# Twelve instead of eight of the last 32 token tiles are summed on TensorE, twenty instead of 24 on VectorE

## The reference

```python
x = x + _L0_ffn_ref(_L0_cond_ref(x, cond_512, ...), ...)      # the last "x +" is the input itself

# inside _L0_ffn_ref:
topv, topi = jax.lax.top_k(glogits, TOPK)                     # TOPK = 4 of E = 32 experts
gw = jax.nn.softmax(topv, axis=-1)
combine = jnp.zeros((N, E), x.dtype).at[jnp.arange(N)[:, None], topi].add(gw)
def body(acc, we):
    wu, wd, ce = we
    ug = h2 @ wu
    u, g = (ug[:, :DFF], ug[:, DFF:])
    return (acc + ce[:, None] * (jax.nn.silu(g) * u @ wd), None)
y2, _ = jax.lax.scan(body, jnp.zeros_like(h2), (W_up, W_down, combine.T))
return x + y2.reshape(Bx, Tx, Dx)
```

## Time and profile before

| | |
|---|---|
| median of 3 runs | 1138.51 us (1137.43 to 1142.05) |
| the profiled execution | 1133.5 us, its span 1131.7 us |
| PE busy in the span | 984.0 us (87%) |
| DVE busy | 829.8 us (73%) |
| POOL busy | 700.9 us (62%) |
| ACT busy | 456.6 us (40%) |
| mean granted TensorE clock | 0.918 of full |
| DMA | 239.22 MB, mean 211 GB/s |

### The profile page before, as it was taken

The page is one execution under the profiler, slowest core; times in us unless marked ns, Lnnn a source line. Parts: engine busy times, 40 slices in busy tenths (PEclk is TensorE's granted clock), DMA queues, the critical chain, the costliest instruction groups (busy, mean ns, idle before and its releaser), DMA issues.

```text
span 1131.7 us, 19754 instructions
## 1 busy us (share of the span) xinstructions
PE 984.0 (87%) x6270; PEld 795.6 (70%) x6270; DVE 829.8 (73%) x1750; ACT 456.6 (40%) x1120; POOL 700.9 (62%) x654
## 2 busy tenths in 40 slices
PE   3879699998999989989987419999999999999995
PEld 2557477676776776757766308888888888888884
DVE  3878589778787788877957526777777677777778
ACT  1123243342432423333344205555555555555541
POOL 1404435757747667576585856777777777777750
PEclk8779799889898898988999659999999999999997
DMA  6237976566566555574665467776776767766599
GB/s 188 69 87 237 326 255 187 157 198 179 176 181 207 161 167 190 179 217 136 186 204 194 154 231 261 266 257 246 255 245 212 250 228 250 257 212 209 133 336 372
DMA packets 110748, 239.22 MB, mean 211 GB/s; under 512 B 19170, under 2 KB 48247, under 8 KB 109914
## 3 DMA queue, kind: packets, MB, share of 16 engines
q1 hardware_dynamic: 84042, 192.03, 51.8%
q0 software_dynamic: 19552, 40.02, 11.1%
q10 hardware_dynamic: 7056, 5.91, 1.6%
HBM read 140.37 MB, written 90.05 MB: 204 GB/s over the span
## 4 chain that ended last, share of the span: by engine, by line
PE 38%; DVE 22%; POOL 18%; issue 14%; DMA 6%; ACT 1%; SPq 0%; DVEq 0%; POOLq 0%; ACTq 0%
POOL rows_in L685 7%; PE gbank L985 7%; PE gbank L852 6%; DVE ring L1354 6%; POOL pick_rows L692 4%; POOL lists L647 4%; PE scores L813 4%; DMA rows_in<-x_rows,token_row 4%; PE gbank L1005 3%; PE gbank L777 3%; PE gbank L748 2%; POOL ring L654 1%; DVE stat L1368 1%; PE gbank L767 1%; DVE prob L1390 1%
## 5 line engine op out<-in xcount | busy, mean ns | idle before, releaser
L985 PE MATMUL gbank<-ring,in_part 128*128 x954 | 262.8, 411 | 0.1
L654 POOL TENSOR_TENSOR ring<-ring 128x512 fp32r<-128x512 f32 x96 | 121.5, 1281 | 141.7 <-ACT ring L1151 141.1
L692 POOL DMA_INDIRECT pick_rows<-rows_out,pair_row x156 | 161.6, 1036 | 56.5 <-issue 46.9
L985 PEld LDWEIGHTS gbank<-ring,in_part 128*128 128x128 f32 x954 | 168.6, 190 | 28.7 <-issue 0.3
L685 POOL DMA_INDIRECT rows_in<-x_rows,token_row x156 | 151.7, 972 | 54.2 <-issue 34.3
L647 POOL DMA_INDIRECT lists<-entry,slot_i x128 | 136.1, 1063 | 36.7 <-issue 34.1
L1005 PE MATMUL gbank<-ring,mid_part 128*128 x954 | 151.3, 294 | 0.4 <-DVE mid_part L1609 0.4
L1588 DVE SCALAR_TENSOR_TENSOR in_part<-scores,norm_w,in_part 128x128 fp32r<-128x128 f32 x318 | 96.8, 346 | 53.2 <-ACT in_part L1196 53.1
L1597 DVE SCALAR_TENSOR_TENSOR mid<-gbank,norms,silu 128x256 f32<-128x256 f32 x156 | 75.5, 484 | 74.4 <-ACT silu L1204 73.0
L852 PE MATMUL gbank<-w_o,ring 128*128 128x256 f32 x512 | 126.3, 403 | 0.6 <-ACT ring L1121 0.6
L777 PE MATMUL gbank<-h_t,w_qk 128*128 128x512 f32 x480 | 122.1, 405 | 4.7 <-DVE ring L1354 2.5
(11 more groups left out here) (171 smaller groups left out, 1553.1 us busy)
## 6 DMA issues: line engine op xcount, KB each, us to landing
w_parts<-ring SPq DMA_DIRECT2D x192, 256.0 KB, 3.2
ring<-w_parts SPq DMA_DIRECT2D x32, 1536.0 KB
ring<-in_W_up SPq DMA_DIRECT2D x64, 256.0 KB, 4.1
q_r<-rot SPq DMA_DIRECT2D x32, 512.0 KB, 6.1
picks<-pick_rows SPq DMA_DIRECT2D x8, 2048.0 KB, 22.2
lists<-in_fill_slots SPq DMA_DIRECT2D x36, 256.0 KB, 5.2
ring<-in_W_down SPq DMA_DIRECT2D x32, 256.0 KB, 3.9
x_t<-in_x_t SPq DMA_DIRECT2D x8, 512.0 KB, 4.9
```

Of the source, the lines that this page charges most:

```text
L654: e.tensor_tensor(lower, lower.bitcast(F32), upper.bitcast(F32), ALU.subtract).then_inc(s_lower, 1)
L692: e.indirect_dma_start(out=pick_rows, out_offset=bass.IndirectOffsetOnAxis(ap=begun_row[:, i:i + 1] if i < AHEAD else pair_row[:, i:i + 1] ...
L985: ins = e.matmul(bank[:, :], in_parts[i % 2][x][:, c, :], ring[:, bass.ds(at + y * WE + c * 2 * DFF, 2 * DFF)], start=k == 0, stop=k == le ...
```

## The change

A list says how many tiles of each part go to TensorE: 1, 2, 1, 2, 1, 2, 1, 2. These are the last tiles of the part (tile 3, or tiles 2 and 3), 12 in all. VectorE takes the first three or the first two. PE and ACT now loop over the 12 tiles, and SP's and VectorE's shapes follow. SP's condition for loading part 6 and 7 counts TensorE's tiles of the parts 0 and 0 to 1: 1 and 3, before 1 and 2.

```diff
+SUMS = [1 + c % 2 for c in range(PARTS)]
+SUMMED = [(c, c * NP + NP - n + k) for c, n in enumerate(SUMS) for k in range(n)]
@@ SP
             if c >= NPICK:
                 w.wait_ge(s_final, c - NPICK + 1)
-                w.wait_ge(s_sum, c - NPICK + 1)
+                w.wait_ge(s_sum, sum(SUMS[:c - NPICK + 1]))
...
-            e.dma_start(d["out"][c * NP * P:(c * NP + NP - 1) * P, :].rearrange("(t p) n -> p t n", p=P),
-                        resid[:, c * NP:c * NP + NP - 1, :]).then_inc(s_out, 16)
-        w.wait_ge(s_out, 16 * 2 * PARTS)
+            own = NP - SUMS[c]
+            e.dma_start(d["out"][c * NP * P:(c * NP + own) * P, :].rearrange("(t p) n -> p t n", p=P),
+                        resid[:, c * NP:c * NP + own, :]).then_inc(s_out, 16)
+        w.wait_ge(s_out, 16 * (PARTS + len(SUMMED)))
@@ PE
-        for c in range(PARTS):
-            bank, t = gbank[c % 2][:, 0:D], c * NP + NP - 1
-            if c >= 2:
-                w.wait_ge(s_summed, c - 1)
+        for n, (c, t) in enumerate(SUMMED):
+            bank = gbank[n % 2][:, 0:D]
+            if n >= 2:
+                w.wait_ge(s_summed, n - 1)
             w.wait_ge(s_resid, NT // NX)
             e.matmul(bank, ident[:, :], resid[:, t, :], start=True, stop=False)
             w.wait_ge(s_picks[c % NPICK], 16 * (c // NPICK + 1))
             for k in range(TOPK):
-                ins = e.matmul(bank, ident[:, :], picks[c % NPICK][:, NP - 1, k, :], start=False, stop=k == TOPK - 1)
+                ins = e.matmul(bank, ident[:, :], picks[c % NPICK][:, t % NP, k, :], start=False, stop=k == TOPK - 1)
             ins.then_inc(s_sum, 1)
@@ ACT
-        for c in range(PARTS):
-            t = c * NP + NP - 1
-            w.wait_ge(s_sum, c + 1)
-            e.activation(resid[:, t, :], gbank[c % 2][:, 0:D], ACT.Copy).then_inc(s_summed, 1)
-            w.wait_ge(s_summed, c + 1)
+        for n, (c, t) in enumerate(SUMMED):
+            w.wait_ge(s_sum, n + 1)
+            e.activation(resid[:, t, :], gbank[n % 2][:, 0:D], ACT.Copy).then_inc(s_summed, 1)
+            w.wait_ge(s_summed, n + 1)
             e.dma_start(d["out"][t * P:(t + 1) * P, :], resid[:, t, :]).then_inc(s_out, 16)
@@ DVE
-            at = slice(c * NP, c * NP + NP - 1)
+            n = NP - SUMS[c]
+            at = slice(c * NP, c * NP + n)
```

More of the change, by code:

```diff
@@ L1634, in vector_program @@
             w.wait_ge(s_picks[c % NPICK], 16 * (c // NPICK + 1))
-            at = slice(c * NP, c * NP + NP - 1)
-            half = own.mark(e.tensor_tensor(pk[:, 0:NP - 1, 0:2, :], pk[:, 0:NP - 1, 0:2, :], pk[:, 0:NP - 1, 2:4, :], ALU.add))
+            n = NP - SUMS[c]
+            at = slice(c * NP, c * NP + n)
+            half = own.mark(e.tensor_tensor(pk[:, 0:n, 0:2, :], pk[:, 0:n, 0:2, :], pk[:, 0:n, 2:4, :], ALU.add))
             w.wait_ge(s_vector, half)
-            whole = own.mark(e.tensor_tensor(pk[:, 0:NP - 1, 0, :], pk[:, 0:NP - 1, 0, :], pk[:, 0:NP - 1, 1, :], ALU.add))
+            whole = own.mark(e.tensor_tensor(pk[:, 0:n, 0, :], pk[:, 0:n, 0, :], pk[:, 0:n, 1, :], ALU.add))
             w.wait_ge(s_back, 16)
             w.wait_ge(s_vector, whole)
-            e.tensor_tensor(resid[:, at, :], resid[:, at, :], pk[:, 0:NP - 1, 0, :], ALU.add).then_inc(s_final, 1)
+            e.tensor_tensor(resid[:, at, :], resid[:, at, :], pk[:, 0:n, 0, :], ALU.add).then_inc(s_final, 1)
     banks_for = banks_of()
```

## The result

The changed kernel takes 1140.03 us (median of 14 runs, 1137.07 to 1148.15) against 1136.99 us for the kernel before (14 runs, 1134.31 to 1142.05): +3.0 us, a ratio of 1.0032 with a 95% interval of 1.0016 to 1.0047. The profiled execution took 1137.89 us, its span 1136.1 us. Forecast were 1142.9 us, +4.4 us, and 1136.1 us for the span.

What follows compares the result with a forecast made beforehand. VectorE and the DMA engines were taken as both at their limit; TensorE would then end last: +5.3 + 0.46 - 1.3 = +4.4 us, 1137.9 against the profiled 1133.5, carried to the median 1142.9 us, range 1138.5 to 1147.

Steps and rivals of the forecast that it cites:

- VectorE saves 4.2 us: VectorE's additions at the end: four parts shrink from three tiles to two, 1.05 us saved each, ending at 1123.5.
- None of the extra tiles fits into TensorE's idle 5.68 us, since ACT is not free: TensorE's third tile: both banks full at 1103.86, it still waits for ACT, and ACT for the scatters.
- Ten tiles behind the release, 4 x 2.16 us on the path less 3.3 of slack: TensorE after ACT's first copy: ten tiles instead of six, ending 8.6 us later at 1133.0, 5.3 past VectorE's old end.
- The last landing, 2.3 us: Final 128 KB output, issued at 1133.45: lands in 2.3 us, bounds 1.7 and 5.2.
- Part 7's load, late but free: SP's load, issued 7.8 us late at about 1113.5, lands at about 1121; cost nothing, bounds 0 to 1.5 us.
- The other signs: ACT's first copy near 1109, ten gapless tiles, final chain through TensorE, load issued at 1113.5 without holding TensorE, DMA full until 1128.
- TensorE wants part 7 at 1130.7: TensorE's eleventh tile needs that load at 1109.54 + 3.86 + 8 x 2.16; even a landing at 1129.8 wouldn't hold TensorE.
- rival (C): Part 7's late load sets the end if landing takes over 17 us; at 20 us, 3 us more, 1146; chance 0.05.
- Sum +4.4 us: Whole kernel: +5.3 for TensorE's tiles, +0.46 to the last issue, -1.3 for the shorter last landing.
- The absolute numbers: Span forecast at 1136.1 us and median time at 1142.9 us, +0.39%.
- Rival (A), clock and release: TensorE's end: another low-clock tile or later release makes it slower by more than 5.7 us; chance 0.25.
- Rival (B), the DMA as the next limit: With ACT's first copy by about 1105, DMA, full until about 1129.5, sets the end; time 1137, not slower; chance 0.10.

Runs made afterwards that it cites:

- early_ones: Changed kernel with TensorE's 12 tiles shared as 1, 1, 2, 1, 2, 1, 2, 2, so part 7's load goes out earlier; ratio 1.0028 to the kernel before.
- pool_wait_12: Changed kernel, 12 tiles on TensorE, with the wait for the last four scatters moved from ACT to POOL; ratio 0.9991 to the kernel before.
- changed kernel again: Changed kernel without any edit, traced and timed a second time as a control; ratio 1.0074 to the kernel before.
- warm: Changed kernel with twelve extra matmuls filling TensorE's wait between its second and third tile; ratio 1.0014 to the kernel before.
- sum10: Changed kernel with ten tiles on TensorE, two of parts 3 and 7, one of each other part; ratio 1.0012 to the kernel before.
- sum16: Changed kernel with sixteen tiles on TensorE, two of each part; ratio 1.0123 to the kernel before.
- sum9: Changed kernel with nine tiles on TensorE, two of the last part, one of each other; ratio 0.9991 to the kernel before.
- dve_only: Kernel before with VectorE taking two tiles of every second part, TensorE still eight, four tiles' sums left out; ratio 1.0003 to the kernel before.
- pool_wait_10: Ten tiles on TensorE, two of parts 6 and 7, with the last scatters' wait on POOL instead of ACT; ratio 0.9997 to the kernel before.
- the two traces of before: Kernel before, unedited, profiled twice as a control; from VectorE's first addition of the end to span end 33.35 and 32.58 us, repeat's ratio 1.0010.
- pool_wait_9: Nine tiles on TensorE, two of the last part, with the last scatters' wait on POOL instead of ACT; ratio 1.0014 to the kernel before.

## Why the prediction was right

- *VectorE saves 4.2 us.* A part of two tiles costs 1.22 + 0.69 + 0.69 us; VectorE without waits (early_ones) ends at 25.04 instead of 29.31, 4.27 us. Right, and of no use, as said.
- *None of the extra tiles fits into TensorE's idle 5.68 us, since ACT is not free.* TensorE is idle 5.34 us at the same place, for ACT. Shown by pool_wait_12: with the wait gone from ACT the idle time goes.
- *Ten tiles behind the release, 4 x 2.16 us on the path less 3.3 of slack.* Ten tiles have nine distances from start to start; eight are 2.15 or 2.16 us, the first is 3.93 (3.86 before). TensorE ends at 1133.50, forecast 1133.0; the whole stage began 0.7 us later. The counts 9, 10 and 16 carry the same line on.
- *The last landing, 2.3 us.* It was 1.7, the lower bound, in this trace and in the five others in which TensorE's last output goes out over 4 us behind VectorE's end (changed kernel again, early_ones, warm, sum10, sum16). Where it is the last by 0.7 to 2.5 us only (sum9, dve_only, pool_wait_12, pool_wait_10) it took 3.2 to 3.7. The term was 0.6 too large. The 2.3 us that the prediction works out from the Trainium skill are stated in the section it names, "Anatomy of one DMA — SWDGE (gpsimd) path" of "DMA: Bandwidth & Descriptors", for DMAs that GpSimd issues; this one is ScalarE's, and the measured 1.7 decides.
- *Part 7's load, late but free.* Issued at 1114.2 (expected 1113.5, with the stage 0.7 later). It landed at 1125.0 and not at 1121. The step "5.2 us and a start" was mis-sized: 10.8 us to landing, just under the lower of the two bounds given (11.0). In the stretch from 1114 to 1120 the DMA engines moved 314 GB/s, and 412 before. VectorE's wait of 3.47 us comes from this, and early_ones shows that it cost nothing. So one sign of being right failed: VectorE was to be done by 1125 with 8 us of room, and was at 1127.7 with 5.8. The other signs came true.
- *TensorE wants part 7 at 1130.7.* This is a slip. From the fourth tile to the eleventh there are seven distances, not eight: 1109.54 + 3.86 + 7 x 2.16 = 1128.5. A load that landed at the upper bound, 1129.8, would have held TensorE by about 1 us, and rival (C) would begin at 15 us to landing and not at 17. The load was down at 1125.0 and the eleventh tile started at 1129.0, so the slip changed nothing here; that "even at 1129.8 TensorE isn't held" was false.
- *Sum +4.4 us.* The two first traces give 37.03 - 33.35 = 3.7 us: 0.6 for the landing, 0.3 for an earlier release, less 0.1 for the third tile. The means of two traces each give 4.5, the first timing 3.0, and the forecast ratio, 1.0039, lies in the first timing's interval (1.0016 to 1.0047) and just below the second's (1.0044 to 1.0104). Both timings lie above 1, so the slowdown is there. Its size in timed runs is open: the first timing puts it inside 0.5%, the second, 1.0074, does not.
- *The absolute numbers.* That the span came out at the forecast 1136.1 us to the tenth is luck: the stage began 0.7 us later than in the kernel before and was 0.7 shorter than forecast. The median was forecast 2.9 us too high: 1.5 because the kernel before measured 1136.99 us in 14 runs and not 1138.51 as in three, and 1.4 because the change measured 3.0 and not 4.4.
- *Rival (A), clock and release.* It is real as a mechanism, and the price of a tile at the low level, 1.7 us, was right: warm gives 1.66. But a second tile at the low level behind the wait, its condition for +6.1, is in none of the ten traces that have the wait on ACT; the third tile alone varies there, from 3.72 to 4.43 us, warm's apart. The changed kernel's own two traces differ by 0.5 us in the third tile and 0.5 in the release, and by 1.0 at the end of the stage. These 0.5 us each don't explain that the second timing, +8.0 us, lies above 5.7. The forecast said that such scatter counts in full only in the changed kernel, and in these traces it does: PE end moves 0.4 us between the two traces of before and VectorE's end not at all, while the 0.8 us of that kernel are those of its last landing.
- *Rival (B), the DMA as the next limit.* Not tested by the change itself. What stood in it as "the same bytes, full until about 1129.5, so no gain beyond 1 to 2 us" held in its size for dve_only, where TensorE's last output was the end, and failed for pool_wait_9 (1.8 to 2.6 us, one trace).

## What to carry to other kernels

Before work is moved from the engine at the limit to one with idle time, look at what the idle time waits for: TensorE's 5.68 us waited for ACT, and ACT for four scatters, so the added tiles went behind the wait and only the 3.3 us at the far end were slack. Slack at the end divided by what both engines change per unit gives the split, here 3.3/(2.16 + 1.06), one tile and not four. A wait that an idle engine can hold as well (here POOL) is best moved there before more work is put behind it: with twelve tiles this took 3.0 to 4.0 us off the end stage, with eight nothing that can be seen, since there TensorE didn't set the end.

## What the hardware showed beyond the forecast

- After an idle time of 5.3 to 6.0 us the first tile on TensorE took 3.72 to 4.43 us in the nine traces that have the wait on ACT and nothing in it, and a tile at the full clock 2.16. The granted clock was 0.50 in most of it in the changed kernel's first trace (3.93 us) and in all of it in the second (4.42). Filling the idle time with matmuls took this to 2.27.
- A 128 KB output took 1.7 us from issue to landing in emptied queues, and 5.2 to 11.0 in the eight of the kernel before, issued into full ones. Part 7's load of 2 MB took 16.2 us queued behind others, 10.8 in the changed kernel's first trace, issued while the DMA share stayed at 0.92 or more, and 9.1 in its second, issued when the share had fallen to 0.08 (1124 to 1125 us).
